# Dense rows of the last layer set partly into the second mean aggregation, with x2 added on TensorE there

## What is computed

```python
def mean_aggr(x):                       # one row for every node
    s = segment_sum(x[src], dst, n)
    return s / maximum(count(dst), 1)[:, None]

x = layernorm(x + L0(x, edge_attr, src, dst))        # messages
x = layernorm(x + L1(x, src, dst))                   # graph attention, gives x2
h = relu(mean_aggr(x) @ W1l.T + b1 + x @ W1r.T)      # first mean aggregation, gives h1
y = mean_aggr(h) @ W2l.T + b2 + h @ W2r.T            # second mean aggregation
x = layernorm(x + y)                                 # gives x3
Q, K = x @ qw, x @ kw                                # projection
alpha = sum(Q[src] * K[dst]) / sqrt(32)              # then softmax over the edges of a destination
...
x = layernorm(x + out_w_layer(aggregate))            # nodes without edges: layernorm(x3 + constant row)
```

## Time and profile before

| | |
|---|---|
| time, median of 3 runs (lowest, highest) | 2895.54 us (2893.41, 2901.38) |
| the profiled execution's own time | 2897.93 us |
| its span | 2896.2 us |
| DVE, PE, ACT, POOL busy | 2309.7, 1832.9, 1740.0, 1695.7 us |
| stage sage2 | about 1938 to 2212 us from the span's start |
| stage att1 | about 2214 to 2534 us |

### The profile page before, as it was taken

How to read it: one execution, slowest core, us unless ns; L and a number is a source line. 1 busy time by engine, 2 the same in 40 slices (tenths; PEclk the granted TensorE clock), 3 DMA queues, 4 the chain that set the end, 5 groups by cost and what they waited for, 6 DMA issues and landing times. The chain is left out here.

```text
span 2896.2 us, 51835 instructions
## 1 busy us (share of the span) xinstructions
PE 1832.9 (63%) x9687; PEld 1401.4 (48%) x9687; DVE 2309.7 (80%) x9110; ACT 1740.0 (60%) x4457; POOL 1695.7 (59%) x1605
## 2 busy tenths in 40 slices
PE   5666666456656653777777666657775666657663
PEld 4655555344545542554455333335664555534442
DVE  7887777798988874788888688857886989888883
ACT  3444445323222233888888688865555888858885
POOL 7777777346666664333333556637775766327675
PEclk8777777688788875899999899988998888757776
DMA  6777767534444435999999789967886888734441
GB/s 179 238 242 229 241 222 234 168 72 79 85 76 79 76 47 171 335 341 345 351 344 347 256 290 300 303 219 235 259 256 206 295 291 292 266 129 166 158 165 52
DMA packets 280171, 625.34 MB, mean 216 GB/s; under 512 B 51230, under 2 KB 84649, under 8 KB 280055
## 3 DMA queue, kind: packets, MB, share of 16 engines
q1 hardware_dynamic: 207543, 523.73, 53.0%
q0 software_dynamic: 72512, 100.52, 15.7%
HBM read 342.76 MB, written 285.23 MB: 217 GB/s over the span
## 5 line engine op out<-in xcount | busy, mean ns | idle before, releaser
L1249 ACT ACTIVATE node_out<-node_in,n_shift,n_root 128x128 f32<-128x128 f32 (+1 forms) x1176 | 468.1, 482 | 80.3 <-DVE n_shift L1563 80.1
L786 POOL DMA_INDIRECT sums<-gat_sums,dst_safe_i x196 | 185.3, 946 | 293.7 <-DVE pre L1979 237.7
L903 POOL DMA_INDIRECT out_dram<-node_x2t,out_index x196 | 209.3, 1068 | 160.0 <-ACT node_x2t L1450 93.7
L794 POOL DMA_INDIRECT src_rows<-x_table,row_i x200 | 201.0, 1005 | 130.6 <-issue 53.8
L786 POOL DMA_INDIRECT src_rows<-in_x_dram,src_i x196 | 195.7, 999 | 84.4 <-issue 83.0
L794 POOL DMA_INDIRECT sums<-x_table,row_i x192 | 192.7, 1004 | 85.9 <-issue 50.0
L849 POOL DMA_INDIRECT gat_sums<-src_rows,add_idx x100 | 160.2, 1602 | 138.6 <-ACT src_rows L1321 45.8
L1546 DVE BATCH_NORM_STATS2 n_stats<-node_in 128x6 f32<-128x256 f32 (+1 forms) x588 | 209.4, 419 | 22.6 <-DMA node_in<-y_nodes 11.6
L1026 PE MATMUL ps<-alpha,node_in 128*128 128x196 f32 x392 | 111.5, 447 | 179.1 <-DVE junk L1869 175.8
L794 POOL DMA_INDIRECT own_rows<-in_x_dram,dst_safe_i x196 | 189.8, 968 | 59.7 <-issue 56.4
L1258 ACT ACTIVATE t_a<-ps 128x512 f32<-128x512 f32 (+1 forms) x198 | 115.9, 585 | 158.8 <-PE ps L948 158.6
(11 more groups left out here) (414 smaller groups left out, 6614.0 us busy)
## 6 DMA issues: line engine op xcount, KB each, us to landing
own_rows<-x_table SPq DMA_DIRECT2D x245, 256.0 KB
node_in<-in_x_dram SPq DMA_DIRECT2D x96, 512.0 KB
x_table<-node_out SPq DMA_DIRECT2D x96, 512.0 KB
x_table<-new_rows SPq DMA_DIRECT2D x147, 256.0 KB
gat_sums<-node_x2t SPq DMA_DIRECT2D x49, 528.0 KB, 4.0
acc_dump<-acc SPq DMA_DIRECT2D x98, 264.0 KB
node_sums<-gat_sums SPq DMA_DIRECT2D x48, 528.0 KB
h_table<-node_h SPq DMA_DIRECT2D x48, 512.0 KB
```

What stands on the lines that cost most here:

```text
L786: g_.indirect_dma_start(out=to[:, g.b, j, 0:width], out_offset=None, in_=tab, in_offset=bass.IndirectOffsetOnAxis(ap=indices(j), axis=0)). ...
L794: g_.indirect_dma_start(out=to4[g.q][:, j, 0:F], out_offset=None, in_=tab, in_offset=bass.IndirectOffsetOnAxis(ap=indices(j), axis=0)).the ...
L903: g_.indirect_dma_start(out=out[:, :], out_offset=bass.IndirectOffsetOnAxis(ap=out_index[:, t:t + 1], axis=0), in_=wide_new[:, g.b, j, :], ...
L1249: last = sc.activation(to[0:pn, g.b, j, :], rows[0:pn, g.b, j, 0:F], ACT.Identity, bias=NORM[k][2][0:pn, g.b, j:j + 1], scale=root[0:pn, j ...
```

## The change

The dense steps of the last layer are split. Twelve of the 49 are set into sage2, one in every fourth iteration (`spaced`); the other 37 stay in att1, in three of every four iterations (`packed`). In sage2 they all use one buffer, in att1 three. In sage2 each of them adds to SP a load and a store, to DVE the stages `last_more`, `last_moments`, `last_inverses` and `last_shifts`, to ACT a root and twice four normalising instructions (in two successive iterations). In sage2 `x3_sums` goes away: PE adds the x2 rows into `ps[3]` by a product with the identity, the moments and the normalised rows are read from `ps[3]`, and `pre` is not used there any more. So `sage_out` now waits for `newd`, given by `new_x3`, where it waited for `pre`, and the load of x2 rows waits for `mm`. The wait for the stores of the stage before (`nodes3`) moves ahead of sage2. In an earlier stage three semaphores are merged into one.

```diff
 L = flow["sage2"]                                   # SP
 wait_all(sp, flow["sage1"]["stored"])
+wait_all(sp, flow["nodes3"]["n_out"])
 ...
-x2_own = load_own(L, L["pre"], x2_table, own2_rows, L["own2"])
+x2_own = load_own(L, L["mm"], x2_table, own2_rows, L["own2"])
-pipeline(sp, STEPS, edges((0, both), (1, dump), (4, store)))
+pipeline(sp, STEPS, edges((0, both)) + [spaced(0, load_last_nodes)] + edges((1, dump), (4, store)) + [spaced(4, store_last_nodes)], per=4)
...
+def load_last_nodes(g):                             # SP; spaced: waits for n_row of the dense step before
+    wait_third_free(sp, D["n_row"], g)
+    ...
+        sp.dma_start(in3[g.b][lo:hi, :, :], node_rows(x3_table, SLOTS, g)[lo:hi]).then_inc(rows_in3.sems[g.b], 16)
...
-pipeline(sp, DENSE_FULL, edges((0, load_own_back(L, x3_table, own_rows))) + [nodes(0, load_nodes(D, x3_table, SLOTS, "n_row"))]
-         + edges((2, store_q)) + [nodes(2, store_nodes(D, out, 0))])
+pipeline(sp, DENSE_FULL, edges((0, load_own_back(L, x3_table, own_rows))) + [packed(0, load_last_nodes)]
+         + edges((2, store_q)) + [packed(2, store_last_nodes)], per=4)
...
 def sage_out(g, jn=J):                              # PE
+    wait_free(pe, L["newd"], g)
+    if g is not FIX:
+        wait_landed(pe, L["own2"], g)
+    own = fix_own[:, 1, :] if g is FIX else own2_rows[:, g.b, :, :].rearrange("p j f -> p (j f)")
+    te.matmul(ps[3][g.b][:, 0:jn * F], ones_bf[:, :], b2_parts[:, 0:jn, :].rearrange("p j f -> p (j f)"),
+              start=True, stop=False)
+    te.matmul(ps[3][g.b][:, 0:jn * F], ident[:, :], own, start=False, stop=False)
     wait_done(pe, L["cp_a"], g)
     wait_done(pe, L["cp_b"], g)
-    wait_free(pe, L["pre"], g)
-    te.matmul(ps[3][g.b][:, 0:jn * F], ones_bf[:, :], b2_parts[:, 0:jn, :].rearrange("p j f -> p (j f)"),
-              start=True, stop=False)
...
-pipeline(act, STEPS, edges((3, new_x3), (2, root), (0, sage_copies)))
+def new_x3(g, jn=J):                                # ACT
+    wait_drained(act, L["stored"], g)
+    wait_done(act, L["e_nm"], g)
+    for j in range(jn):
+        last = sc.activation(new_rows[:, g.b, j, :], ps[3][g.b][:, j * F:(j + 1) * F], ACT.Identity, ...)
+    last.then_inc(L["newd"].sem, 1)
+pipeline(act, STEPS, edges((3, new_x3), (2, root)) + [spaced(2, last_node_root)] + edges((0, sage_copies))
+         + [spaced(3, last_node_rows(0, J)), spaced(4, last_node_rows(J, DJ))], per=4)
...
-run[0], (2, x3_sums), run[1], (2, x3_moments), run[2], run[3], (0, means)), per=4)
+pipeline(dve, STEPS, edges((3, x3_shifts)) + [spaced(3, last_inverses), spaced(3, last_shifts)]
+         + edges((0, sources_landed), run[0], run[1], (2, x3_moments), run[2], run[3], (0, means))
+         + [spaced(1, last_more), spaced(2, last_moments)], per=4)
...
+pipeline(dve, DENSE_FULL, edges(spread[0]) + [packed(1, last_inverses)] + edges(spread[1]) + [packed(1, last_shifts)]
+         + edges(spread[2], (2, products), spread[3], (2, score_sums)) + [packed(0, last_more), packed(0, last_moments)], per=4)
```

More of the change, by code:

```diff
@@ L200, in at @@
                 stage(step(s - lag))
[L202 removed]
+    first = (longest + 3) // 2 * 2 if per == 2 else (longest + 6) // 4 * 4
     loops = (looped - first) // per
@@ L895, in _ @@
             L = flow["att2"]
-            wait_all(pool, flow["nodes4"]["n_out"])
+            for b in range(3):
+                pool.wait_ge(rows_out3.sems[b], rows_out3.end[b])
             def scatter_rows(g):
@@ L1251, in make, with last_node_root, last_node_rows @@
                     last.then_inc(L[made].sem, 1)
+                return make
+            def last_node_root(g):
+                D, at = flow["nodes4"], root3[g.b][0:dense_p(g), :]
+                wait_done(act, D["n_ve"], g)
+                sc.activation(at, at, ACT.Sqrt).then_inc(D["n_rt"].sem, 1)
+            def last_node_rows(lo, hi):
+                def make(g):
+                    D, pn = flow["nodes4"], dense_p(g)
+                    if lo == 0:
+                        wait_third_drained(act, rows_out3, g)
+                        wait_done(act, D["n_nm"], g)
+                    for j in range(lo, hi):
+                        last = sc.activation(out3[g.b][0:pn, j, :], in3[g.b][0:pn, j, :], ACT.Identity,
+                                             bias=shift3[g.b][0:pn, j:j + 1], scale=root3[g.b][0:pn, j:j + 1])
+                    if hi == DJ:
+                        last.then_inc(D["n_row"].sem, 1)
                 return make
@@ L1394, in _ @@
             L = flow["sage2"]
-            new_x3, root = normed_rows(L, "e", pre, new_rows, "newd", "stored"), roots(L, "e")
-            pipeline(act, STEPS, edges((3, new_x3), (2, root), (0, sage_copies)))
+            root = roots(L, "e")
+            def new_x3(g, jn=J):
+                wait_drained(act, L["stored"], g)
+                wait_done(act, L["e_nm"], g)
+                for j in range(jn):
+                    last = sc.activation(new_rows[:, g.b, j, :], ps[3][g.b][:, j * F:(j + 1) * F], ACT.Identity,
+                                         bias=NORM["e"][2][:, g.b, j:j + 1], scale=NORM["e"][1][:, g.b, j:j + 1])
+                last.then_inc(L["newd"].sem, 1)
+            pipeline(act, STEPS, edges((3, new_x3), (2, root)) + [spaced(2, last_node_root)] + edges((0, sage_copies))
+                     + [spaced(3, last_node_rows(0, J)), spaced(4, last_node_rows(J, DJ))], per=4)
             sage_copies(FIX, 1)
@@ L1428, in _ @@
             L = flow["att2"]
-            wait_all(act, flow["nodes4"]["n_out"])
+            for b in range(3):
+                act.wait_ge(rows_out3.sems[b], rows_out3.end[b])
             def silu(g, jn=WJ):
@@ L2079, in _, with x3_moments @@
             L = flow["sage2"]
[L2081 to L2084, removed]
+            def x3_moments(g, jn=J):
                 wait_done(dve, L["mm"], g)
-                wait_free(dve, L["newd"], g)
-                v.tensor_tensor(pre[:, g.b, 0:jn, :].rearrange("p j f -> p (j f)"), ps[3][g.b][:, 0:jn * F],
-                                own, ALU.add).then_inc(L["pre"].sem, 1)
@@ L2090, in x3_moments @@
-            def x3_moments(g, jn=J):
-                wait_done(dve, L["pre"], g)
-                moments((L, "e", g, pre, P, jn))
+                wait_free(dve, L["e_nm"], g)
+                for j in range(0, jn, 2):
+                    last = v.bn_stats(NORM["e"][0][:, g.b, j:j + 2, :].rearrange("p j c -> p (j c)"),
+                                      ps[3][g.b][:, j * F:(j + 2) * F].rearrange("p (j f) -> p f j", f=F))
+                last.then_inc(L["e_bn"].sem, 1)
+                variances(L, "e", g, P, jn, NORM["e"][1][:, g.b, :])
```

125 lines of the change are left out of this document (89 added, 36 removed).

## The result

The changed kernel takes 3114.88 us (median of four runs, 3110.28 to 3136.57) against 2897.22 us for the kernel before (four runs, 2893.41 to 2901.38): 1.0766 times as long, with a 95% interval of 1.0713 to 1.0819. Forecast were 3112 us. The profiled execution took 3110.28 us, with a span of 3108.6 us, 212.4 us more than before.

What follows compares the result with a forecast made beforehand. No engine full in sage2, its step set by POOL's gathers and a loop through SP; DVE bounds att1. 253 us more in sage2, 37 less in att1, on 2897.9: 3114, predicted 3112 us; range 2985 to 3190.

Steps and rivals of the forecast that it cites:

- The ring: Sage2: sage_out, transposes, copies, new_x3, next sage_out follow one another each step; 7.0 us at full clock, 8.2 us taken.
- Rival 2: Sage2: the ring doesn't bind, POOL's pace sets 5.01 us a step; 2861 us in all; chance 0.07.
- rival 1: Sage2: the ring at full clock, store's landing mostly hidden; 7.0 us a step, 3008 us in all; chance 0.17.
- the clock: PE in sage2: a granted clock of 0.81, adding 1.25 us a step to the ring.
- Rival 3: Sage2: the ring at half clock throughout, 10.3 us a step; 3214 us in all; chance 0.07.
- The dense rows on ACT: ACT in sage2: 24 normalising halves of 1.6 us for the twelve dense steps, on the ring; 38 us.
- the stall: Sage2: ACT's new_x3 waits for a store stuck behind SP's waiting dense load; 11 x 6.0 = 66 us.
- Sage2 in sum: Whole sage2 stage: 49 x 8.2 + 38 + 66 = 506 us against 253 us, 253 us more.
- Att1: Att1 stage: twelve of 49 steps lose 2.99 us of DVE work; 5.5 us a step, 37 us less.
- the lower bound of the forecast: Att1 stage: only 13 us less, if light and heavy steps don't even out (6.0 us a step).
- At nothing: Costed at nothing: moved nodes3 wait, merged semaphores, waits for last dense stores, ACT's root in sage2, removal of x3_sums.
- The rule on bursts: TensorE, from the Trainium skill: bursts each start at the low clock after a wait; would make Rival 3 likelier.

Runs made afterwards that it cites:

- second: Changed kernel with x2 added on DVE again (x3_sums and pre back, sage_out waiting for pre), dense steps kept in sage2; 3009.03 us.
- third: Changed kernel with SP issuing the dense load behind the dump and the store of the same iteration; 3107.28 us.
- fourth experiment: Changed kernel with four PSUM banks for sage_out, so that it waits for newd of step s - 4; 2989.78 us.
- the last two kernels: Changed kernel with four banks, two dense buffers, later att1 stores, root behind the copies, 2898.95 us; the same with x2 on DVE and two banks, 2940.64 us.
- the first experiment: Kernel before with only x2 moved to PE by the identity product, sage_out waiting for newd, all dense steps in att1; 3001.62 us.
- the last but one kernel: Changed kernel with four banks, two dense buffers, later att1 stores and ACT's root moved behind sage_copies; 2898.95 us.
- the two cures: Changed kernel with four PSUM banks for sage_out, 2989.78 us, and with two dense buffers and later stores in sage2, 3083.49 us; both together 2913.11 us.

## Why the prediction was right, and where its steps were off

**The ring: right.** PE waits for `new_x3` 46 times, idle while ACT makes it; one experiment builds the ring alone (106 us) and one opens it in the changed kernel (132 us). Rival 2, that it doesn't bind, is out, and so is rival 1: the clock did not stay as it was. Rival 3, half clock throughout, would have been 12.4 us a step with its other terms (609 / 49); it was 9.89.

**Its length: over-sized, and the clock under-sized.** The ring is 6.4 us at full clock, by the single step and by the run with spare products, where I had 7.0. In that step the transposes start 3.06 us after the bias product (forecast 2.44 + 0.9 = 3.34). The identity product itself was sized well, 0.96 us from its start to the next (2158.56 to 2159.52); the products behind it take 1.78 us to the transposes, where the step of the earlier trace rows had 2.13:

```profile
2052.62 0.49 PE L1149 MATMUL ps<-w2l_t,t_a 128*128 128x128 f32 x2
```

From the transposes to the next bias product it is 3.33 us (forecast 3.66): `new_x3`, which now reads PSUM, takes 1.50 us in place of 1.65, and PE starts 0.13 us after it. The forecast's 0.24 us for that hand-over was misread: the row at 2056.84 names `pre`, not ACT's copy, as what PE waited for. The clock was 0.75, not 0.81: by the forecast's formula 0.5 x 0.8 x 4.1 = 1.64 us a step in place of 1.25.

**The dense rows on ACT and the stall: right in size.** The halves last 1.64 us, as costed, and stand between the copies and `new_x3`. ACT waited 63.3 us for the store in 11 places, where 66 us were forecast, by the mechanism forecast: the store stuck behind the waiting load, landing 4.4 us after its issue. The late dump hid behind it, as forecast: in the place shown DVE's wait for it ends at 2150.10, ACT's for the store at 2150.68. What the forecast lacks is that such a term has no fixed worth. Taken away in the ring it gave 35 us, with the ring open 83 us.

**Sage2 in sum.** By measured terms: 6.4 + 1.64 + 0.8 + 63.3 / 49 = 10.1 us a step, 9.89 measured; forecast were 506 / 49 = 10.3. The stage cost 227 us more in place of 253: the shorter ring (29 us) outweighs the lower clock (19 us), the stage before was some 4 us longer between its bias products than 49 x 5.16 us, and the 12 us by which this sum exceeds the measured stage were not traced.

**Att1: half of what was forecast.** 19 us less in place of 37, 5.86 us a step in place of 5.5. The rounded average of heavy and light steps did not come out, as the lower bound of the forecast had allowed. One cause is shown: own-row loads stood behind SP's wait to store q, and later stores brought 5.91 down to 5.74 us, 8 us of the 18 that were missing. The rest is open.

**The two misses offset each other.** Sage2 cost 26 us less than forecast and att1 gave 18 us less; that leaves 8 us, and sage2's later begin gives them back. That the total is off by 3 us is luck: its steps were off by 26 and 18 us. The later begin is scatter as far as the runs show: the last dense store of the stage before was issued at 1934.06 us in place of 1928.43, but at 1942.31, 1948.53 and 1940.01 us in the second, third and fourth experiment, whose programs are the changed kernel's up to there. So no price can be read for the merged semaphores, which I had costed at nothing. The moved wait was covered: from that store to the first load of sage2 it is 9.8 us after and 9.5 us before.

**At nothing.** The root of the dense rows was free, as costed, by cover of the ring (17.6 us of waiting in all); with the ring open ACT waited 35 us there, which moving it showed to be slack too. The removal of `x3_sums` was also costed at nothing, and under the ring no run shows it to be worth anything; with the ring open it may be part of the 36 us by which the last two kernels differ in sage2, which was not taken apart.

**The rule on bursts** that stood in rival 3 (the Trainium skill, TensorE: Matmul & The Clock Gate, HAM oscillation) has each burst begin at the low clock after a wait; the waits of the page's example are longer than the gaps here, so it spoke less for this rival than the forecast says. Here, after gaps of the same 2.29 us, the bias product took 0.60 us in one step of the first experiment and 0.38 us in two others: the trace agrees in part. With each burst at the low clock the kernel would have needed 3214 us.

## What to carry to other kernels

A stage in which no engine is full has no room to give until one knows which ring of waits sets its step: a buffer of two that is released at the far end of another engine's list closes such a ring, and four of them open it (9.89 and 7.21 us a step here). In SP's program, which issues its DMAs in order, a load that waited for its buffer stopped every store behind it (63.3 us of ACT's waiting in 11 places), so a shared queue wants loads whose buffer is surely free; moving the load behind the stores did not help as long as the buffer was single. Take terms that share a ring out together before you judge one of them: alone, the two cures gave 132 and 35 us, together 215.

## What the runs showed of the hardware

The granted clock can be bought: with five idle products a step, 1.24 us of work in gaps of 2.3 us or more, it went from 0.84 to 1.00 and the kernel from 3002 to 2958 us. I had expected a clock below 0.85 in the ring, but not that filling half of the gap would bring it to full.

In the last but one kernel, where the ring is open, each of the twelve dense additions of sage2 had one gather beside it that took longer than the others, 1.16 to 1.95 us. The longest of them, with its addition:

```profile
2099.79 1.21 DVE L2235 TENSOR_TENSOR node_in<-node_in,local_bc 128x1024 f32<-128x1024 f32 x1
...
2099.87 1.95 POOL L898 DMA_INDIRECT src_rows<-h_table,row_i  x1 [0.30 <-issue]
```

The gathers of that stage with no addition beside them averaged 0.95 us, and none took more than 1.3; in the first experiment, which has no such addition in sage2, none did either. Together the twelve cost 6.6 us in the stage, less than the 10 us that the one gather of 1.77 us had led me to price.
